# A three-stage graph kernel on one core: the last four tiles of the last quarter in 384 and 128 columns instead of 256 and 256, and the closing work in groups of 4, 3 and 1 row blocks instead of 4, 2 and 2

## The chip, the core and the metric

One core of a Trainium2 chip runs the kernel. The metric is the time of one execution on the device in microseconds (us); the figure for a kernel is the median of its runs.

## What is computed

The input is a node table x of 4096 x 128 and an adjacency matrix of 4096 x 4096, both float32, with small weights. Cut to what matters:

```python
def conv(x, a, eps, W, b):
    ax = a @ x
    h = ax + (1.0 + eps[0]) * ax
    for i in range(3):
        h = relu(h @ W[i].T + b[i])
    return h
merged = concatenate((conv(x, adj, ...), conv(x2, adj, ...)), axis=1)
x = layernorm(x + merged @ Wm.T + bm)
A_hat = adj + eye(4096)
d = where(deg > 0, rsqrt(deg), 0)          # deg: row sums of A_hat
x = layernorm(x + (d[:, None] * A_hat * d[None, :]) @ x @ W.T + b)
```

The second layer is the one that matters here: a product of the whole matrix with a 4096 x 128 table, a 128 x 128 projection, a residual and a layer norm over each row.

## The kernel before

**Tiling.** The 4096 output rows are cut into four quarters of 1024 rows (QUARTERS, QW). The products are made transposed: the stationary operand is a 128 x 128 block of the table, the moving operand is a stretch of the matrix, 128 contraction rows by up to 512 output rows (CW), and a PSUM bank `ps[...]` collects 128 features by 512 output rows. The words "columns" below are columns of the moving operand, so output rows of the result. A matrix tile in SBUF is 128 x 1024. To keep float32 accuracy, every operand is split into a rounded high part and the rest: ScalarE (ACT) rounds a tile into `ahi` or `hhi` (L626), VectorE (DVE) subtracts to get `alo` or `alo_extra` (L791), and TensorE (PE) makes three products, high by high, low by high and high by low, all in the type float32r, each with its own weight load.

**Order of the work.** Each engine has one instruction stream, written out by hand, and semaphores join them. First come four quarters of layer 0 (aggregation, three dense layers, merge), then four of layer 1. While a quarter of a layer streams its 32 tiles, the closing work of the quarter before is interleaved at fixed tile numbers. The matrix tiles arrive through SyncE's queue (SP) into a ring.

**The last quarter.** Here nothing follows that could hide the closing work, so the order is another one (`last_quarter` in the tensor stream). The 1024 output rows are two chunks of 512. Tiles 0 to 15 hold all 32 contraction blocks for the first chunk, two blocks per tile, tiles 16 to 31 the same for the second chunk, so `unit_products` (L524) issues 2 x 3 = 6 matmuls per tile. The first chunk is closed at tile 16 and projected (`project`, L510) while the second one streams. The last four tiles (SPLIT = 4) are walked through twice. The first walk ("half 0") takes their first TW columns and finishes output rows 0 to TW-1 of the chunk in `ps3`. The second walk ("half 1") takes the other columns, in a fresh bank `ps0`; since `ps3` already holds those columns of the tiles before, ACT copies both parts out (L758 for the first TW columns, L759 for the rest) and DVE adds `ps0` to the second part at the end (L1055, once per block of 128).

**The closing work** runs on row blocks of 128, eight in a quarter. TAIL names three groups: group 0 is the first chunk (blocks 0 to 3), group 1 the blocks that half 0 finishes, group 2 those that half 1 finishes. PE projects group 1 between the first and the second tile of half 1, and group 2 one block at a time after the add of L1055. DVE then does, for each group: `z` (L1061) per block, the statistics (L1066, L872) per block, and the variance plus epsilon (`vareps`, L879). GpSimd (POOL) raises it to the power -0.5 (`rstd`, L1090). For groups 0 and 1 DVE makes a shift (`nshift`, L884), ACT writes the normalised blocks into `outn` (L764) and SP stores them (L410). For group 2 DVE does the last step itself (L1075). The order in the DVE stream is fixed: group 1 up to its `vareps`, the shift of group 0, the add of L1055, the shift of group 1, then group 2:

```python
            for g, (k0, k1) in enumerate(TAIL):
                if g == 2:
                    ...
                    for k in range(k0, k1):
                        at = (k - HB) * P
                        dve.tensor_tensor(h[:, 1, at:at + P], ps[0][:, at - TW:at - TW + P], h[:, 1, at:at + P],
                                          ALU.add).then_inc(ay_added, 1)
                    shifts(2 * QUARTERS + 1, slice(*TAIL[1]))
```

Of the kernel before, what the change touches and what calls it, by code (L numbers as in the profile page):

```python
# [27 lines left out]
P = 128  # L28
# [7 lines left out]
CW = 512  # L36
# [9 lines left out]

QUADS = tuple((0, 1, LAST * 2 + c) + tuple(m for m in range(2, JB // 4) if m != LAST * 2 + c) for c in range(CH))
HALF_UNITS = JB // CH
TW = CW // 2

TAIL = ((0, 4), (4, 6), (6, 8))
TINY = 1.1754944e-38


# [58 lines left out]
def build(nc, a_t, head, early, x12, params, out):  # L113
    with ExitStack() as ctx:  # L114
# [3 lines left out]
        def sem(name):  # L118
            return ctx.enter_context(nc.semaphore(name))
# [50 lines left out]
        ps = [ctx.enter_context(nc.psum_tensor(f"ps{i}", [P, CW], F32)) for i in range(M)]  # L170
        pd = ctx.enter_context(nc.psum_tensor("pd", [P, M, CW], F32))
        merged = pd[:, 0:2, :].rearrange("p c (k d) -> p (c k) d", d=P)

        merged_last = lambda k: pd[:, 1 + max(k + 1 - TAIL[2][0], 0), (k % 4) * P:(k % 4 + 1) * P] if k >= HB else merged[:, k, :]
        totals = pd[:, 2, 0:QW // TB]
# [51 lines left out]
        out_written = sem("out_written")  # L227
        tail_ready = [sem(f"tail_ready{g}") for g in range(len(TAIL))]
        tail_written = sem("tail_written")
# [42 lines left out]
        def unit(n):  # L272

            c, i = n // HALF_UNITS, n % HALF_UNITS
            return c, 4 * QUADS[c][i // 2] + 2 * (i % 2)
# [23 lines left out]
        def ring_hi(layer, q, n):  # L299

            i = slot(layer, q, n)
            if i >= SPLIT:
                m = 2 * (i - SPLIT)
                return hhi[:, m:m + 2, :].rearrange("p m w -> p (m w)")
            return ahi[:, i, :]

        def ring_lo(layer, q, n):

            i = slot(layer, q, n)
            return alo_extra[:, i - SPLIT, :] if i >= SPLIT else alo[:, i, :]  # L310
# [24 lines left out]
        def _(sp):  # L335
# [63 lines left out]
            for m in range(PAIRS):  # L399
# [5 lines left out]
                for r, done in enumerate((unit_in[s], landed)):  # L405
                    sp.dma_start(dst[:, r, :].rearrange("p (t w) -> p t w", w=CW),
                                 a_t[pair + r][:, :, c * CW:(c + 1) * CW]).then_inc(done, 16)
            for g, (k0, k1) in enumerate(TAIL):
                sp.wait_ge(tail_ready[g], 1)
                sp.dma_start(out[LAST][:, k0 * P:k1 * P], outn[:, k0 * P:k1 * P]).then_inc(tail_written, 16)  # L410
            sp.wait_ge(tail_written, 16 * len(TAIL))


        @block.tensor
        def _(pe):
# [88 lines left out]
            def project(q, chunks=CH, blocks=range(KB)):  # L504

                wait(pe, ay_copied, q * CH + chunks)
                pe.wait_ge(z_ready, q + QUARTERS)
                for k in blocks:
                    to, first = (merged_last(k), blocks[0]) if q is LAST else (merged[:, k, :], k - k % 4)
                    mm = pe.matmul(to, h[:, k // 4, (k % 4) * P:(k % 4 + 1) * P],  # L510
                                   par[:, WO_AT:WO_AT + P], start=(k == first),
                                   stop=(k % 4 == 3 or k == blocks[-1]), skip_group_check=True)
                mm.then_inc(project_done, 1)

            def unit_products(n, cols, open_bank, bank, opens, closes):

                c, j = unit(n)
                hi, lo = ring_hi(1, LAST, n), ring_lo(1, LAST, n)
                for t in range(2):
                    at = slice(t * CW + cols.start, t * CW + cols.stop)  # L520
                    for k, (w, a) in enumerate(((x1hi, hi), (x1lo, hi), (x1hi, lo))):
                        if open_bank and t == 0 and k == 2:
                            pe.wait_ge(lo_ready, (QUARTERS + LAST) * JB + n + 1)
                        mm = pe.matmul(bank, block_of(w, j + t), a[:, at], start=(n == opens and t == 0 and k == 0),  # L524
                                       stop=(n == closes and t == 1 and k == 2), skip_group_check=True)
                return mm

            def last_quarter():

                for n in range(JB - SPLIT):  # L530
                    c = n // HALF_UNITS
                    pe.wait_ge(hi_ready, (QUARTERS + LAST) * JB + n + 1)
                    if n % HALF_UNITS == 0:
                        pe.wait_ge(ay_copied, (LAST - 2) * CH + c + 1)
                    mm = unit_products(n, slice(0, CW), True, ps[CH + c][:, :], c * HALF_UNITS, (c + 1) * HALF_UNITS - 1)
                    mm.then_inc(block_used, 1)
                    if n == PE_PROJECT:
                        project(LAST - 1)
                    if n == HALF_UNITS + PE_PROJECT + 1:
                        project(LAST, 1, range(KB // CH))  # L540
                for half in range(2):
                    for n in range(JB - SPLIT, JB):
                        if half == 0:
                            pe.wait_ge(hi_ready, (QUARTERS + LAST) * JB + n + 1)
                        mm = unit_products(n, slice(half * TW, (half + 1) * TW), half == 0, ps[(3, 0)[half]][:, 0:TW],
                                           (None, JB - SPLIT)[half], JB - 1)
                        if half:
                            mm.then_inc(block_used, 1)
                            if n == JB - SPLIT:
                                project(LAST, 2, range(*TAIL[1]))  # L550
                    if half == 0:
                        mm.then_inc(ay_done, 1)
# [27 lines left out]
            for q in range(1, QUARTERS - 1):  # L580
                layer1_quarter(q, q - 1)
            last_quarter()
            for i, k in enumerate(range(*TAIL[2])):
                pe.wait_ge(ay_added, i + 1)
# [4 lines left out]
        def _(act):  # L589
# [167 lines left out]
            act.wait_ge(ay_done, LAST + 1)  # L757
            act.activation(h[:, 1, 0:TW], ps[3][:, 0:TW], ACT.Copy).then_inc(ay_copied, 1)  # L758
            act.activation(h[:, 1, TW:CW], ps[3][:, TW:CW], ACT.Copy).then_inc(ay_copied, 1)  # L759
            act.wait_ge(out_written, 16 * LAST)  # L760
# [9 lines left out]
        def _(dve):  # L770
# [278 lines left out]
            for g, (k0, k1) in enumerate(TAIL):  # L1049
                if g == 2:  # L1050
                    dve.wait_ge(ay_copied, LAST * CH + 3)
                    dve.wait_ge(block_used, 2 * QUARTERS * JB)
# [4 lines that stand above are left out]
# [103 lines left out]
```

## Time and profile before

| | us |
|---|---|
| median of three runs | 594.59 (594.35 to 595.46) |
| the profiled execution | 595.34 |
| its span in the trace | 593.5 |
| PE busy | 586.1 (99%) |
| DVE busy | 540.0 (91%) |
| ACT busy | 372.8 (63%) |
| POOL busy | 28.7 (5%) |

The profiled execution is 1.84 us longer than its span, which is what lies around the traced instructions. Times of day in the rows are microseconds from the start of the span. A matmul's row in a timeline has its start and the time from there to its modelled end; since matmuls overlap, the distance between two starts says what one costs in a stream. A row with a count (x4) merges instructions, and its time runs from the first start to the last end.

### The profile page before, as it was taken

What the parts mean: (1) busy time and instruction counts of PE and PEld (TensorE: products, weight loads), DVE (VectorE), ACT (ScalarE), POOL (GpSimd) and SP (SyncE); (2) the same over time, 40 slices, a digit from 0 to 9 for tenths busy, and PEclk for the clock granted to TensorE, in tenths of its full rate; (3) what the DMA queues carried; (4) which work ended last, traced back from release to release, by engine and by line L of the source; (5) the groups of instructions that cost most, each with busy time, mean ns of one, the idle gap of its engine ahead of it and who ended that gap; (6) DMA issues with size and microseconds to landing.
All of it is one profiled execution on the core that took longest, in us unless ns stands there. A gap on an engine that the chain in (4) does not pass through costs nothing.

```text
span 593.5 us, 7715 instructions
## 1 busy us (share of the span) xinstructions
PE 586.1 (99%) x2676; PEld 484.6 (82%) x2676; DVE 540.0 (91%) x677; ACT 372.8 (63%) x494; POOL 28.7 (5%) x31
## 2 busy tenths in 40 slices
PE   8999999999999999999999999999999999999996
PEld 7788888888888888888888888867888888888885
DVE  5999999997987998898799999995899999989986
ACT  6643537752454773363667336476897888898893
POOL 1000000001100000110000020000200010010011
PEclk9999999999999999999999999999999999999998
DMA  8967665444555543454534475775699999999911
GB/s 331 391 246 284 213 214 212 142 142 142 197 180 194 175 172 145 141 188 173 204 141 141 142 273 185 286 306 224 238 358 407 354 362 390 401 362 375 388 48 71
DMA packets 27833, 141.56 MB, mean 239 GB/s; under 512 B 2592, under 2 KB 3360, under 8 KB 13600
## 3 DMA queue, kind: packets, MB, share of 16 engines
q1 hardware_dynamic: 27104, 139.41, 63.2%
q10 hardware_dynamic: 704, 1.84, 0.8%
q8 instruction: 14, 0.23, 0.2%
q14 instruction: 11, 0.09, 0.0%
HBM read 139.14 MB, written 2.10 MB: 238 GB/s over the span
## 4 chain that ended last, share of the span: by engine, by line
PE 94%; DVE 4%; DMA 1%; issue 0%; ACT 0%; SPq 0%; POOLq 0%; POOL 0%; DVEq 0%
PE ps L448 77%; PE ps L524 7%; PE pd L466 6%; PE pd L477 2%; DVE alo L791 1%; PE pd L510 1%; DMA raw<-early 1%; DVE rowsum L802 1%; DVE rowsum L806 1%; DVE x2s L775 0%; DVE x1lo L775 0%; DVE rowsum L799 0%; ACT ahi L626 0%; SPq L347 0%; POOLq L114 0%
## 5 line engine op out<-in xcount | busy, mean ns | idle before, releaser
L626 ACT ACTIVATE ahi<-raw 128x1024 fp32r<-128x1024 f32 x213 | 223.1, 1057 | 170.1 <-PE ps L448 156.0
L791 DVE TENSOR_TENSOR alo<-raw,ahi 128x1024 fp32r<-128x1024 f32 x213 | 257.9, 1218 | 31.6 <-ACT ahi L626 29.8
L448 PE MATMUL ps<-ahi,x2s 128*128 128x512 f32 x512 | 138.2, 389 | 0.0
L448 PE MATMUL ps<-ahi,x1hi 128*128 128x512 f32 x384 | 122.1, 394 | 0.5 <-ACT ahi L605 0.3
L448 PE MATMUL ps<-ahi,x1lo 128*128 128x512 f32 x384 | 120.5, 390 | 0.0
L448 PE MATMUL ps<-alo,x1hi 128*128 128x512 f32 x384 | 120.3, 389 | 0.0
L448 PEld LDWEIGHTS ps<-ahi,x2s 128*128 128x128 f32 x512 | 96.1, 188 | 20.1
L448 PEld LDWEIGHTS ps<-ahi,x1hi 128*128 128x128 f32 x384 | 71.8, 188 | 17.2 <-DVE x2s L775 1.4
L448 PEld LDWEIGHTS ps<-alo,x1hi 128*128 128x128 f32 x384 | 72.2, 188 | 15.2 <-DVE alo L783 0.2
L448 PEld LDWEIGHTS ps<-ahi,x1lo 128*128 128x128 f32 x384 | 72.2, 188 | 15.0
L448 PE MATMUL ps<-alo,x2s 128*128 128x512 f32 x256 | 80.1, 389 | 0.0
L802 DVE TENSOR_TENSOR rowsum<-rowsum,raw 128x1024 f32<-128x1024 f32 x60 | 72.9, 1215 | 0.0
L806 DVE TENSOR_TENSOR rowsum<-rowsum,raw 128x1024 f32<-128x1024 f32 x56 | 68.0, 1215 | 0.0
L791 DVE TENSOR_TENSOR alo_extra<-raw,hhi 128x1024 fp32r<-128x1024 f32 x42 | 50.6, 1219 | 6.8 <-ACT hhi L626 6.4
L448 PEld LDWEIGHTS ps<-alo,x2s 128*128 128x128 f32 x256 | 48.0, 188 | 10.0
L626 ACT ACTIVATE hhi<-raw 128x1024 fp32r<-128x1024 f32 x42 | 43.6, 1052 | 9.4 <-PE ps L448 8.2
L1090 POOL TENSOR_TENSOR rstd<-vareps,halves 128x8 f32<-128x8 f32 (+2 forms) x10 | 19.4, 1937 | 251.4 <-DVE vareps L985 145.1
L647 ACT ACTIVATE h<-pd,par 128x512 f32<-128x512 f32 x48 | 31.1, 680 | 0.4 <-PE pd L466 0.3
L811 DVE TENSOR_TENSOR hlo<-h,hhi 128x512 fp32r<-128x512 f32 x36 | 22.6, 681 | 0.0
L631 ACT ACTIVATE hhi<-h 128x512 fp32r<-128x512 f32 x36 | 22.1, 629 | 0.8
L1085 POOL TENSOR_TENSOR degpow<-degc,halves 128x8 f32<-128x8 f32 x4 | 6.7, 1670 | 309.0 <-DVE degpos L850 309.0
L448 PE MATMUL ps<-hhi,x1hi 128*128 128x512 f32 x64 | 20.6, 398 | 0.0
(97 smaller groups left out, 507.9 us busy)
## 6 DMA issues: line engine op xcount, KB each, us to landing
raw<-a_t SPq DMA_DIRECT2D x108, 1024.0 KB, 4.9
raw<-a_t SPq DMA_DIRECT2D x32, 512.0 KB, 7.3
raw<-early SPq DMA_DIRECT2D x7, 512.0 KB, 8.3
xn<-x SPq DMA_DIRECT2D x3, 1024.0 KB, 8.6
out<-outn ACTq DMA_DIRECT2D x3, 512.0 KB, 6.8
par<-params SPq DMA_DIRECT2D x1, 708.0 KB, 13.5
raw<-head SPq DMA_DIRECT2D x2, 256.0 KB, 3.3
xn<-x SPq DMA_DIRECT2D x1, 512.0 KB, 8.3
```

Of the source, the lines that this page charges most:

```text
L448: mm = pe.matmul(ps[bank + (CH * (q % 2) if layer else 0)][:, :], block_of(w, n), a[c], start=(n == 0 and k == 0), stop=(n == JB - 1 and k ...
L466: mm = pe.matmul(pd[:, m, :], w[:, at:at + P], a[:, m, :], start=(k == 0), stop=(k == len(passes) - 1))
L477: mm = pe.matmul(merged[:, k, :], h[:, CH * b + k // 4, (k % 4) * P:(k % 4 + 1) * P], par[:, WM_AT + b * P:WM_AT + (b + 1) * P], start=(k ...
L524: mm = pe.matmul(bank, block_of(w, j + t), a[:, at], start=(n == opens and t == 0 and k == 0), stop=(n == closes and t == 1 and k == 2), s ...
L626: act.activation(ring_hi(layer, q, n), raw_tile(layer, n), ACT.Copy).then_inc(hi_ready, 1)
L631: act.activation(hhi[:, m, :], h[:, m, :], ACT.Copy).then_inc(hhi_ready, 1)
L647: act.activation(h[:, m, :], pd[:, m, :], ACT.Relu, bias=par[:, at:at + 1]).then_inc(h_ready, 1)
L791: dve.tensor_tensor(ring_lo(layer, q, n), raw_tile(layer, n), as_f32(ring_hi(layer, q, n)), ALU.subtract).then_inc(lo_ready, 1)
L802: dve.tensor_tensor(rowsum[:, :], rowsum[:, :], tile, ALU.add).then_inc(rowsum_step, 1)
L806: dve.tensor_tensor(to[:, :], rowsum[:, :], tile, ALU.add).then_inc(raw_used, 1)
L811: dve.tensor_tensor(hlo[:, m, :], h[:, m, :], as_f32(hhi[:, m, :]), ALU.subtract).then_inc(hlo_ready, 1)
L1090: pool.tensor_tensor(rstd[:, r], vareps[:, r], halves[:, r], ALU.pow).then_inc(rstd_ready, 1)
```

## The change

TW becomes 384, so half 0 takes 384 columns of the last four tiles and half 1 takes 128. TAIL becomes (0, 4), (4, 7), (7, 8), so group 1 has three row blocks and group 2 has one. The tensor stream's slices follow these two sizes.

```diff
-TW = CW // 2
-
-TAIL = ((0, 4), (4, 6), (6, 8))
+TW = CW - P
+
+TAIL = ((0, 4), (4, 7), (7, 8))
@@ last_quarter
-                        mm = unit_products(n, slice(half * TW, (half + 1) * TW), half == 0, ps[(3, 0)[half]][:, 0:TW],
+                        mm = unit_products(n, slice(*((0, TW), (TW, CW))[half]), half == 0, ps[(3, 0)[half]][:, 0:(TW, CW - TW)[half]],
                                            (None, JB - SPLIT)[half], JB - 1)
```

On PE, around the projection of group 1 in half 1 (`pd<-par,h` is the projection), before:

```order
L524 MATMUL ps<-alo_extra,x1hi 128x256
L510 MATMUL pd<-par,h 128x128 x2
L524 MATMUL ps<-hhi,x1hi 128x256
L524 MATMUL ps<-hhi,x1lo 128x256
L524 MATMUL ps<-alo_extra,x1hi 128x256
```

and now:

```order
L524 MATMUL ps<-alo_extra,x1hi 128x128
L510 MATMUL pd<-par,h 128x128 x3
L524 MATMUL ps<-hhi,x1hi 128x128
L524 MATMUL ps<-hhi,x1lo 128x128
L524 MATMUL ps<-alo_extra,x1hi 128x128
```

The 24 matmuls of half 1 have half the columns, and one projection has moved from the very end into the middle of the walk. The 24 of half 0 read 128x384 in place of 128x256.

On DVE, from group 1 to the end of the program, before:

```order
L1061 SCALAR_TENSOR_TENSOR z<-pd,dall,xn 128x128 x2
L1066 BN_STATS stats<-z 128x6 x2
L872 BN_AGGR mv<-stats 128x2 x2
L879 TENSOR_SCALAR vareps<-mv 128x2
L884 SCALAR_TENSOR_TENSOR nshift<-mv,rstd 128x4
L1055 TENSOR_TENSOR h<-ps,h 128x128 x2
L884 SCALAR_TENSOR_TENSOR nshift<-mv,rstd 128x2
L1061 SCALAR_TENSOR_TENSOR z<-pd,dall,xn 128x128 x2
L1066 BN_STATS stats<-z 128x6 x2
L872 BN_AGGR mv<-stats 128x2 x2
L879 TENSOR_SCALAR vareps<-mv 128x2
L1075 TENSOR_SCALAR outn<-z,mv,rstd 128x128 x2
```

and now:

```order
L1061 SCALAR_TENSOR_TENSOR z<-pd,dall,xn 128x128 x3
L1066 BN_STATS stats<-z 128x6 x3
L872 BN_AGGR mv<-stats 128x2 x3
L879 TENSOR_SCALAR vareps<-mv 128x3
L884 SCALAR_TENSOR_TENSOR nshift<-mv,rstd 128x4
L1055 TENSOR_TENSOR h<-ps,h 128x128
L884 SCALAR_TENSOR_TENSOR nshift<-mv,rstd 128x3
L1061 SCALAR_TENSOR_TENSOR z<-pd,dall,xn 128x128
L1066 BN_STATS stats<-z 128x6
L872 BN_AGGR mv<-stats 128x2
L879 TENSOR_SCALAR vareps<-mv 128x1
L1075 TENSOR_SCALAR outn<-z,mv,rstd 128x128
```

One block's instructions have moved from behind the add of L1055 to ahead of it. On ACT seven blocks are normalised in place of six, and the two copies are 384 and 128 wide. The stores of groups 1 and 2 have 192 KB and 64 KB in place of 128 KB each.

## Rows read from the trace of the kernel before

**Rows 1.** Chain of waits, two pieces: start us, us, what.

```profile
540.41 2.72 PE ps L524 x12
...
587.69 2.35 issue
```

**Rows 2.** Timeline of PE, last four tiles: start us, us, engine line op out<-in.

```profile
581.04 0.28 PE L524 MATMUL ps<-hhi,x1hi 128*128 128x256 f32 x1
...
583.91 0.28 PE L524 MATMUL ps<-hhi,x1hi 128*128 128x256 f32 x1
...
584.63 0.63 PE L510 MATMUL pd<-par,h 128*128 128x128 f32 x4
...
585.22 0.28 PE L524 MATMUL ps<-hhi,x1lo 128*128 128x256 f32 x1
...
587.12 0.28 PE L524 MATMUL ps<-alo,x1hi 128*128 128x256 f32 x1
```

**Rows 3.** Timeline of PE and its weight loads, merge of layer 0, quarter 0.

```profile
132.66 1.08 PEld L477 LDWEIGHTS pd<-par,h 128*128 128x128 f32 x9
...
132.55 0.19 PE L474 MATMUL pd<-partial,same_place 128*128 128x32 f32 x1
...
132.57 0.28 PE L474 MATMUL pd<-partial,same_place 128*128 128x32 f32 x1
```

**Rows 4.** Chain of waits, the merge of layer 0, quarter 0.

```profile
132.85 3.65 PE pd L477 x32
```

**Rows 5.** Timeline of ACT, copies out of PSUM and the last normalisation.

```profile
565.78 0.58 ACT L741 ACTIVATE h<-ps 128x512 f32<-128x512 f32 x1
...
584.11 0.38 ACT L758 ACTIVATE h<-ps 128x256 f32<-128x256 f32 x1 [2.86 <-PE ps L524]
...
587.07 2.42 ACT L764 ACTIVATE outn<-z,nshift,rstd 128x128 f32<-128x128 f32 x6 [2.30 <-DVE nshift L884]
```

**Rows 6.** Timeline of DVE, closing work; idle before and its releaser in brackets.

```profile
582.43 1.12 DVE L1061 SCALAR_TENSOR_TENSOR z<-pd,dall,xn 128x128 f32<-128x128 f32 x4
...
584.91 0.17 DVE L879 TENSOR_SCALAR vareps<-mv 128x4 f32<-128x4 f32 x1
585.30 0.61 DVE L1061 SCALAR_TENSOR_TENSOR z<-pd,dall,xn 128x128 f32<-128x128 f32 x2 [0.22 <-PE pd L510]
...
586.74 0.17 DVE L879 TENSOR_SCALAR vareps<-mv 128x2 f32<-128x2 f32 x1
586.82 0.15 DVE L884 SCALAR_TENSOR_TENSOR nshift<-mv,rstd 128x4 f32<-128x4 f32 x1
587.51 0.49 DVE L1055 TENSOR_TENSOR h<-ps,h 128x128 f32<-128x128 f32 x2 [0.54 <-PE ps L524]
587.92 0.15 DVE L884 SCALAR_TENSOR_TENSOR nshift<-mv,rstd 128x2 f32<-128x2 f32 x1
588.38 0.61 DVE L1061 SCALAR_TENSOR_TENSOR z<-pd,dall,xn 128x128 f32<-128x128 f32 x2 [0.32 <-PE pd L510]
...
589.83 0.17 DVE L879 TENSOR_SCALAR vareps<-mv 128x2 f32<-128x2 f32 x1
590.81 0.60 DVE L1075 TENSOR_SCALAR outn<-z,mv,rstd 128x128 f32<-128x128 f32 x2 [0.81 <-POOL rstd L1090]
```

**Rows 7.** Timeline of POOL, the powers of groups 0 and 1.

```profile
585.16 1.01 POOL L1090 TENSOR_TENSOR rstd<-vareps,halves 128x4 f32<-128x4 f32 x1 [12.13 <-DVE vareps L879]
586.99 0.70 POOL L1090 TENSOR_TENSOR rstd<-vareps,halves 128x2 f32<-128x2 f32 x1 [0.83 <-DVE vareps L879]
```

**Rows 8.** SP's last issue in the timeline; stores with KB each and us to landing.

```profile
591.44 0.33 SPq L410 DMA_DIRECT2D out<-outn  x1
...
out<-outn SPq DMA_DIRECT2D x1, 256.0 KB, 2.1
out<-outn SPq DMA_DIRECT2D x2, 128.0 KB, 1.7
```

**Rows 9.** Busy time in a stretch: us, engines busy (count), granted clock, DMA, GB/s.

```profile
588.00:588.60 0.60, 0.57 (x4) 0.38 (x4) 0.28 (x2) 0.60 (x2) 0.00 (x0) 1.00 0.00 0
```

## The prediction

> **What bounds the kernel now.** The page's shares come first: PE is busy for 99% of the span, so only two things can move the time, the columns that PE streams and the closing work that starts when PE has stopped. The change leaves every matmul of the program in place up to the last four tiles, so I read only the last 13 us. The chain of waits is the next view. It walks PE until the projection of group 1 and then shows a piece of 2.35 us called issue, in which nothing is released [rows 1]. That piece is the warning: the chain took a side path (group 1's power on POOL), and the engines' timelines must say what really happened there. They do. The last matmul of half 1 starts at 587.12 [rows 2]; DVE, idle for 0.54 us, starts the add of L1055 at 587.51 with PE as its releaser, `z` of group 2 at 588.38 after the projection, `vareps` at 589.83 and the final normalisation at 590.81 [rows 6]; SP issues the last store at 591.44, and it needs 1.7 us to land [rows 8]. So today the end hangs on PE: add at 587.51, then 3.93 us to the issue. DVE had finished group 1 at 586.74 + 0.17 = 586.91 and the shift of group 0 by 586.97 [rows 6]: it was early by about half a microsecond. That slack is what the change spends.
>
> **PE, half 0.** A 512-column matmul costs 2.72 / 12 = 0.227 us in a stream [rows 1], one with 256 columns (583.91 - 581.04) / 24 = 0.120 us [rows 2]. The line through both gives 0.173 us for 384. Half 0 starts at 581.04 and ends its issue at 581.04 + 24 x 0.173 = 585.2.
>
> **PE, half 1.** No float32r matmul with 128 columns is in the trace, so its price is bounded. Below: the line through 512 and 256 gives 0.066 us. Above: a float32 matmul with 128 columns is two passes, 32 passes in 3.65 us [rows 4], so 0.114 each and 0.23 per matmul. Between them stands the weight load, one per matmul. In the merge nine loads take 1.08 us, and with the 0.19 us of one taken off, eight distances of 0.111 us [rows 3]. That it is the load and not the stream is seen at the two passes with only 32 columns: they end at 132.55 + 0.19 = 132.74 and 132.57 + 0.28 = 132.85, again 0.11 apart [rows 3]. I take 0.115, between this pace and today's 0.120: halving the columns frees next to nothing. The Trainium skill (TensorE: Matmul & The Clock Gate, "Back-to-back issue gap") gives about 81 ns for a sustained stream of load and matmul pairs at 128 columns; the load pace of this trace speaks against so low a value for 4-byte weights. By that figure PE would be done 0.6 us sooner than I say, and the time would be the same, for DVE is then the only bound; it makes the tie below safer.
>
> The projection of group 1 now waits for a 384-column copy. ACT starts it 0.20 us after half 0 (583.91 to 584.11 now) at 585.4; between 0.38 for 256 columns and 0.58 for 512 I take 0.48 [rows 5]; PE follows 0.14 after its end, at 586.0. The first tile of half 1 has been issued by 585.2 + 6 x 0.115 = 585.9, so PE stands still for 0.1. From there: four passes took 585.22 - 584.63 - 0.12 = 0.47 us [rows 2], six take 0.70; the other 18 matmuls take 18 x 0.115 = 2.07; PE has issued all at 588.8, against 587.24 now. The add follows 0.27 later (587.24 to 587.51), less 0.05 for the shorter last stream: **589.0 by PE**.
>
> **DVE, group 1.** From the start of the projection to `z` it takes 0.67 us (584.63 to 585.30), and two more passes 0.22: `z` at 586.9. From `z` to `vareps` two blocks need 586.74 - 585.30 = 1.44 and four 584.91 - 582.43 = 2.48 [rows 6], so 0.52 a block and 1.96 for three: `vareps` at 588.87, the shift of group 0 at 588.95, and the add can start at **589.03 by DVE**. Both engines come to the same instant, 1.5 us later than now. A quicker stream on PE would therefore gain nothing: the slack of half a microsecond is gone, and DVE is what is late next.
>
> **A new wait.** Behind the add DVE has the shift of group 1, which needs `rstd`. POOL starts 0.25 after `vareps` (586.74 to 586.99), takes 0.70 for two columns and 1.01 for four, so 0.85 for three [rows 7]: 588.87 + 0.25 + 0.85 = 589.97, and the shift starts at 590.0. Today it starts right behind the adds at 587.92 [rows 6] with `rstd` there since 587.69. Queued behind it in DVE's stream is `z` of group 2, which PE has ready at 589.03 + 0.87 = 589.9 but which now starts at 590.1, one step of 0.08 behind the shift. Now it is 588.38: **+1.7**.
>
> **What the last group saves.** One block less: 0.52 up to `vareps`, (1.01 - 0.70) / 2 = 0.16 on POOL, and (0.60 - 0.34) = 0.26 of the last normalisation, whose single instruction takes about 0.34 like each `z`; together 0.94 us. The second add is not in this sum: it ran beside the first projection. So the last block is ready at 591.41 + 1.7 - 0.94 = 592.2, against 591.41.
>
> **ACT and the stores.** ACT starts the normalisations 0.25 after the shift of group 0 (586.82 to 587.07 now), so at 589.2. Six take 2.42 us; with 0.48 for the last, 0.39 apart [rows 5]. Seven are done at 589.2 + 6 x 0.39 + 0.48 = 592.0, where now they are done at 589.49, far ahead of everything. So SP issues group 1's store at 592.05 and is occupied for 0.33 us [rows 8]; the last store, ready at 592.2, is issued at 592.4. 256 KB land in 2.1 us and 128 KB in 1.7 [rows 8]; by that slope 64 KB need 1.5 and 192 KB 1.9: both land near 593.9. Counted as one transfer of 256 KB from 592.05 it would be 594.15. Today the last one lands at 591.44 + 1.7 = 593.14. I take +0.85 us, with ends of +0.7 and +1.0 from these two counts. The Trainium skill (DMA: Bandwidth & Descriptors, the two cost components of an issued DMA) has about 2.0 us whatever the size, plus bytes / 436 GB/s. The rows disagree with its constant (1.7 us for 128 KB, all told) and agree that size matters little; with its slope the halved last store is 0.15 us shorter, not 0.2, which would put the sum 0.05 higher.
>
> Edits without a price: the clock stays granted in full while PE projects the last group (1.00 from 588.00 to 588.60 [rows 9]), and the gap before that projection is no longer than now. ACT's second copy (L759) is narrower and done long before the add. Group 0 is untouched until the shift.
>
> **The sum** stands against the profiled execution, 595.34 us with a span of 593.5: the span becomes about 594.35 and that execution 596.2. The median of the runs is 0.75 lower than the profiled one, so the median goes from 594.59 to 595.4. I call a difference under 0.2%, 1.19 us, no difference; that is about what a measurement of this kernel can tell. The forecast is +0.14%, on the slower side of no difference. With 0.120 per matmul instead of 0.115, and the ends of the store, this case reaches from 594.9 to 596.0.
>
> **Rivals.**
> A. Narrow matmuls are dear (the slower side). If float32r with 128 columns costs what float32 costs, 0.228 us, half 1 decides: first tile done at 586.6, projections 0.70, 18 x 0.228 = 4.1, add at 591.6, `z` at 592.5, the issue 2.1 later at 594.6 against 591.44, stores no longer on each other's heels and the last one 0.2 shorter: +3.0, so 597.6. It decides as soon as the add comes later than 590.1 - 0.87 = 589.2, which is at 0.125 us per matmul. For it: nothing in the trace shows float32r narrower than 256 columns, and the nearest form of 128 columns, float32, does cost that. Against: up to there its price falls in line with the columns, and the load pace gives no reason for a rise.
> B. ACT does not keep its pace of 0.39 between normalisations, or two stores at once cost more than one of 256 KB. At 0.48 each, seven end at 592.56, the stores are issued at 592.6 and 592.95 and land at 594.5: +1.4, 596.0. For it: ACT and DVE then work at the same time on `z` and `outn`. Against: they do so now, and the pace is 0.39.
> C. The saving comes through. With 0.066 per matmul PE's add would come at 588.2; if DVE were also there by then, the sum is +0.7 - 0.94 and a little for the store: 594.3, and 593.4 if the add did not move at all. Against: DVE would have to do 1.96 us of group 1 in 1.2, and each step of it is in the rows.
> D. The change does not act (the groups reach the end as before): 594.6. The order of instructions speaks against it.
>
> **Chances.** Forecast 0.62, A 0.18, B 0.13, C 0.05, D 0.02. The range of 594.3 to 596.8 leaves out A and the far end of C, 0.2. Faster by over 0.2% needs C in full: 0.03. No difference: 0.54 of the forecast's 0.62, 0.03 of B, 0.02 of C, D, together 0.61. Slower: 0.08 of the forecast (its high end passes 595.78), A, 0.10 of B: 0.36.
>
> **What would show it.** In the profile after: starts in half 0 0.173 apart; in half 1 0.11 to 0.12; `z` of group 1 near 586.9 with three blocks; the add near 589.0 with next to no idle time before it; the shift of group 1 idle before it, released by POOL; `z` of group 2 at 590.1; SP's last two issues back to back near 592.2. The prediction is wrong if half 1's matmuls stand 0.2 apart, if the add comes before 588.5, or if the shift of group 1 doesn't wait.

## The result and the profile after

| | before | after |
|---|---|---|
| median, 20 runs each, us | 595.06 (594.35 to 595.76) | 596.15 (595.71 to 597.31) |
| ratio | | 1.002, 95% interval 1.0013 to 1.0026 |
| span of the profiled execution, us | 593.5 | 594.0 |
| first matmul of half 0, from the start | 581.04 | 580.43 |
| from there to the span's end, from unrounded times | 12.51 | 13.55 |

The change costs 1.1 us, 0.2%. The forecast was +0.8 (0.14%) from a median of 594.59, to 595.4; the measured 596.15 lies in the range given, 0.75 above the point.

The last two lines of the table carry the comparison. The two programs do the same work up to the first matmul of half 0, yet it stands 0.61 us earlier in the trace of the changed kernel. The chain of waits of each kernel shows a difference of the same size at the start of the program, in the first load: 5.38 us in the changed kernel and 5.99 in the kernel before.

```profile
1.67 5.38 DMA raw<-early
```

```profile
1.67 5.99 DMA raw<-early
```

(The first line is from the kernel after, the second from the kernel before.) So two spans may differ by half a microsecond for a reason that has nothing to do with the change. From here on I count from the first matmul of half 0 and call the distance to the span's end the **tail**: 12.51 before, 13.55 after, +1.04. The views print a span to 0.1 us only, and from such spans the two would be 12.46 and 13.57, the figures that the expectations below go by; the tails in this text are taken from the trace's own unrounded times.

The timeline of PE after (start us, us, engine line op), the first matmuls of half 0, of half 1, and the last one:

```profile
580.43 0.33 PE L524 MATMUL ps<-hhi,x1hi 128*128 128x384 f32 x1
...
584.61 0.22 PE L524 MATMUL ps<-hhi,x1hi 128*128 128x128 f32 x1
584.67 0.27 PE L524 MATMUL ps<-hhi,x1lo 128*128 128x128 f32 x1
584.78 0.27 PE L524 MATMUL ps<-alo_extra,x1hi 128*128 128x128 f32 x1
584.89 0.28 PE L524 MATMUL ps<-hhi,x1hi 128*128 128x128 f32 x1
585.00 0.28 PE L524 MATMUL ps<-hhi,x1lo 128*128 128x128 f32 x1
585.12 0.27 PE L524 MATMUL ps<-alo_extra,x1hi 128*128 128x128 f32 x1
585.35 0.94 PE L510 MATMUL pd<-par,h 128*128 128x128 f32 x6
...
587.98 0.27 PE L524 MATMUL ps<-alo,x1hi 128*128 128x128 f32 x1
```

Half 0 takes (584.61 - 580.43) / 24 = 0.174 us a matmul, half 1 0.111, against 0.120 for either before [rows 2].

The first two matmuls of half 1 stand only 0.06 us apart, so 128 columns need no more than that. The timeline of the weight loads (PEld) shows what the later ones keep step with:

```profile
584.61 0.19 PEld L524 LDWEIGHTS ps<-hhi,x1lo 128*128 128x128 f32 x1
584.72 0.19 PEld L524 LDWEIGHTS ps<-alo_extra,x1hi 128*128 128x128 f32 x1
584.83 0.19 PEld L524 LDWEIGHTS ps<-hhi,x1hi 128*128 128x128 f32 x1
```

The loads begin 0.11 us apart, and each matmul begins 0.06 behind its own load (584.61 and 584.67, 584.72 and 584.78).

The timeline of DVE after, to be held against [rows 6]; the brackets say how long DVE was idle and who ended it:

```profile
586.33 0.87 DVE L1061 SCALAR_TENSOR_TENSOR z<-pd,dall,xn 128x128 f32<-128x128 f32 x3 [1.86 <-PE pd L510]
587.23 0.68 DVE L1066 BATCH_NORM_STATS2 stats<-z 128x6 f32<-128x128 f32 x3
587.94 0.31 DVE L872 BATCH_NORM_AGGREGATE mv<-stats 128x2 f32<-128x6 f32 x3
588.29 0.17 DVE L879 TENSOR_SCALAR vareps<-mv 128x3 f32<-128x3 f32 x1
588.37 0.15 DVE L884 SCALAR_TENSOR_TENSOR nshift<-mv,rstd 128x4 f32<-128x4 f32 x1
588.44 0.28 DVE L1055 TENSOR_TENSOR h<-ps,h 128x128 f32<-128x128 f32 x1
589.42 0.16 DVE L884 SCALAR_TENSOR_TENSOR nshift<-mv,rstd 128x3 f32<-128x3 f32 x1 [0.70 <-POOL rstd L1090]
589.50 0.35 DVE L1061 SCALAR_TENSOR_TENSOR z<-pd,dall,xn 128x128 f32<-128x128 f32 x1
590.43 0.15 DVE L879 TENSOR_SCALAR vareps<-mv 128x1 f32<-128x1 f32 x1
591.25 0.35 DVE L1075 TENSOR_SCALAR outn<-z,mv,rstd 128x128 f32<-128x128 f32 x1 [0.66 <-POOL rstd L1090]
```

The add of L1055 has lost its bracket: DVE goes into it without idle time, where PE ended 0.54 us of it before. The shift of group 1 has gained one, released by POOL. The idle time was moved, not removed.

ACT, and SP's last two issues in their timelines; then the stores with the time to landing:

```profile
588.62 2.80 ACT L764 ACTIVATE outn<-z,nshift,rstd 128x128 f32<-128x128 f32 x7 [3.15 <-DVE nshift L884]
```

```profile
591.45 0.35 SPq L410 DMA_DIRECT2D out<-outn  x1
591.84 0.43 SPq L410 DMA_DIRECT2D out<-outn  x1
```

```profile
out<-outn SPq DMA_DIRECT2D x1, 192.0 KB, 1.9
out<-outn SPq DMA_DIRECT2D x1, 64.0 KB, 1.7
```

The last block is ready at 591.25 + 0.35 = 591.60, the last issue comes 0.24 us later, behind the one for group 1. The last store lands 1.04 us later than before, counted from half 0; 1.01 of it is the later issue (11.41 against 10.40).

### The profile page after: what moved, and what is told of

It reads as the page before. It is cut to its first block, busy times and chain, and to the rows that moved or that the text cites. A ratio compares the mean times of both kernels' runs of the same rounds, so it can differ in the third digit from the quotient of the medians.

```text
span 594.0 us, 7713 instructions
## 1 busy us (share of the span) xinstructions
PE 586.7 (99%) x2676; PEld 485.4 (82%) x2676; DVE 539.6 (91%) x675; ACT 372.9 (63%) x495; POOL 28.7 (5%) x31
## 4 chain that ended last, share of the span: by engine, by line
PE 94%; DVE 4%; DMA 1%; issue 0%; ACT 0%; POOL 0%; SPq 0%; POOLq 0%
PE ps L448 77%; PE ps L524 7%; PE pd L466 6%; PE pd L477 2%; DVE alo L791 1%; PE pd L510 1%; DMA raw<-early 1%; DVE rowsum L802 1%; DVE rowsum L806 1%; DVE x2s L775 0%; DVE x1lo L775 0%; DVE rowsum L799 0%; ACT ahi L626 0%; DVE z L1061 0%; POOL rstd L1090 0%
## 5 line engine op out<-in xcount | busy, mean ns | idle before, releaser
L1090 POOL TENSOR_TENSOR rstd<-vareps,halves 128x8 f32<-128x8 f32 (+3 forms) x10 | 19.4, 1938 | 252.4 <-DVE vareps L985 145.1
```

The source lines that it names most:

```text
L1090: pool.tensor_tensor(rstd[:, r], vareps[:, r], halves[:, r], ALU.pow).then_inc(rstd_ready, 1)
```

## The experiments

The differences looked for are tenths of a microsecond, and the start of the program moves by more than that, so beside each ratio to the kernel before I give the tail of the profiled execution. Such tails repeat closely: the kernel before and before_more, whose last issue is at the same place, both have 12.51, and the kernel after, after_cut and narrow64 have 13.55, 13.55 and 13.56. Each run below the first two has 7 to 11 executions (narrow64 one), and its ratio is to executions of the kernel before made beside it, whose medians were 594.97 to 595.09. before_cut, after_cut and narrow64 leave out a part of the products, so their output is not that of the full work.

| kernel | median us, ratio to before (95%) | add at | z of last group | last issue | tail |
|---|---|---|---|---|---|
| before | 595.06 | 6.47 | 7.34 | 10.40 | 12.51 |
| after | 596.15, 1.002 (1.0013 to 1.0026) | 8.01 | 9.07 | 11.41 | 13.55 |
| before_cut | 594.48, 0.9993 (0.9983 to 1.0002) | 5.86 | 6.76 | 9.81 | 11.92 |
| after_cut | 596.03, 1.0017 (1.0008 to 1.0027) | 8.01 | 9.07 | 11.41 | 13.55 |
| before_more | 595.04, 0.9997 (0.9987 to 1.0007) | 6.47 | 7.34 | 10.40 | 12.51 |
| after_more | 596.19, 1.0024 (1.0012 to 1.0035) | 8.59 | 9.66 | 12.00 | 14.14 |
| late_shift | 596.43, 1.0019 (1.001 to 1.0028) | 8.01 | 8.88 | 11.41 | 13.56 |
| act_store | 596.17, 1.0017 (1.0008 to 1.0026) | 8.01 | 9.07 | 11.18 | 13.56 |
| both_moves | 596.06, 1.0013 (1.0004 to 1.0023) | 8.02 | 8.88 | 11.00 | 13.51 |
| cols_alone | 596.15, 1.0019 (1.001 to 1.0028) | 7.93 | 8.81 | 11.60 | 13.71 |
| narrow64 | 596.20, one execution | 8.01 | 9.08 | 11.41 | 13.56 |
| early_shift | 595.78, 1.0015 (1.0005 to 1.0024) | 7.95 | 9.08 | 11.19 | 13.18 |
| early_late | 595.76, 1.001 (1.0001 to 1.0019) | 7.94 | 8.82 | 10.96 | 13.09 |
| pool_norm | 595.27, 1.0002 (0.9993 to 1.0011) | 6.47 | 7.34 | 10.74 | 12.85 |

### Who holds the add: less work on PE, more on DVE

The first pair leaves out 8 of half 1's 24 matmuls, those with the low part of the table, in the kernel before and in the changed one (`skip` is a new argument of `unit_products`, empty elsewhere).

```diff
                     for k, (w, a) in enumerate(((x1hi, hi), (x1lo, hi), (x1hi, lo))):
+                        if k in skip:
+                            continue
...
-                                           (None, JB - SPLIT)[half], JB - 1)
+                                           (None, JB - SPLIT)[half], JB - 1, (1,) if half else ())
```

> The kernel before, half 1 without its products of the low part of the table (8 of its 24 matmuls of 256 columns are left out, so the last rows lose a part of their accuracy). Times are counted from the first matmul of half 0; in the kernel before, the add of L1055 starts at 6.47, z of the last group at 7.34, the last store is issued at 10.40 and the span ends at 12.46. If PE sets the end there and DVE is early by half a microsecond, the add moves until DVE's order stops it: to 6.0, z to 6.87, the issue to 9.93, and the time falls by 0.5 us against before. If something behind PE sets the end, nothing moves.

> The changed kernel with the same 8 matmuls of half 1 left out (128 columns each). In the changed kernel the add starts at 8.01, the shift of group 1 at 8.99, z of the last group at 9.07, the last issue is at 11.41 and the span ends at 13.57. Main theory: DVE's work on three blocks and POOL's power hold the end, PE is only level with them; PE ends some 0.8 us sooner and nothing else moves, 0.0 us against the changed kernel. Rival: the narrow matmuls are what costs the time; then the add comes up to 0.8 us sooner and the time falls by 0.5 or more.

The timeline of DVE, before_cut:

```profile
586.90 0.16 DVE L886 SCALAR_TENSOR_TENSOR nshift<-mv,rstd 128x4 f32<-128x4 f32 x1
586.98 0.48 DVE L1057 TENSOR_TENSOR h<-ps,h 128x128 f32<-128x128 f32 x2
587.80 0.16 DVE L886 SCALAR_TENSOR_TENSOR nshift<-mv,rstd 128x2 f32<-128x2 f32 x1 [0.35 <-POOL rstd L1092]
```

In the kernel before, the add moved from 6.47 to 5.86 and stopped where DVE's order stopped it, right behind the shift of group 0; and at once the wait for POOL appeared that the change also has. The tail fell by 0.59, the median by 0.49 (594.97 beside it). In the changed kernel the last matmul of half 1 came at 6.88 instead of 7.55, and no other time moved: add 8.01, tail 13.55. PE does not hold the end there.

The second pair makes group 1's statistics twice.

```diff
+                if g == 1:
+                    for k in range(k0, k1):
+                        dve.bn_stats(partial[:, 6 * (k - k0):6 * (k - k0) + 6], z[:, k, :])
                 for k in range(k0, k1):
                     dve.bn_stats(stats[:, k, :], z[:, k, :]).then_inc(stats_step, 1)
```

> The kernel before with group 1's statistics made twice on DVE (the first time into a tile that nothing reads): 2 x 0.19 = 0.38 us more ahead of the add. Main theory: DVE has half a microsecond of slack there, so the add stays at 6.47 and the time is that of before, +0.0. Rival (DVE's work in the tail adds up whatever PE does): +0.38 us.

> The changed kernel with group 1's statistics made twice: 3 x 0.19 = 0.57 us more on DVE ahead of the add. Main theory: no slack is left, the add, the shift of group 1 and everything behind come 0.57 us later: add at 8.6, z of the last group at 9.65, last issue at 12.0, and the time is 0.55 us above the changed kernel. Rival (PE sets the end): +0.1 or less, since PE and DVE would have to differ by half a microsecond.

The same extra work is free in one kernel (add at 6.47, last issue at 10.4, both as before) and costs its full length in the other (add, z and last issue 0.58 or 0.59 later, tail +0.59). The medians do not show it: the expected 0.55 us is missing there, after_more's median is 0.04 above the changed kernel's and 0.16 above that of after_cut, which ran beside it. Its seven executions lie between 595.73 and 597.16, and the profiled one, the fastest, reached half 0 at 579.80, 0.63 us before the changed kernel's. So the two theories are told apart by the trace alone.

### What the waits behind the add cost

```diff
-                    shifts(2 * QUARTERS + 1, slice(*TAIL[1]))
...
                 i.then_inc(z_ready, 1)
+                if g == 2:
+                    shifts(2 * QUARTERS + 1, slice(*TAIL[1]))
```

> The changed kernel with one instruction moved on DVE: the shift of group 1 stands behind z of the last group instead of ahead of it, so z no longer waits for POOL. z of the last group comes at 8.88 instead of 9.07 from the first matmul of half 0, and the last block is ready 0.19 us sooner. Theory of the stores (SP is still busy with group 1's store until 11.37): the last issue stays near 11.4 and the time is the same, 0.0. Theory of the chain on DVE: the last issue moves to 11.2 and the time falls by 0.19 us.

The timeline of DVE, late_shift:

```profile
589.74 0.35 DVE L1060 SCALAR_TENSOR_TENSOR z<-pd,dall,xn 128x128 f32<-128x128 f32 x1 [0.58 <-PE pd L510]
590.00 0.15 DVE L884 SCALAR_TENSOR_TENSOR nshift<-mv,rstd 128x3 f32<-128x3 f32 x1
```

z is now released by PE and comes at 8.88, as worked out, and the last block is ready 0.20 sooner. The tail is 13.56, the same. The gain ended at SP:

```profile
591.88 0.82 SPq L410 DMA_DIRECT2D out<-outn  x2
```

The two issues stand in one piece of 0.82 us, so the last one waits for the one before it (591.88 is 11.02 from half 0, where ACT has finished its seventh block).

```diff
             for g, (k0, k1) in enumerate(TAIL):
+                if g == 1:
+                    continue
                 sp.wait_ge(tail_ready[g], 1)
...
+            act.wait_ge(tail_ready[1], 1)
+            k0, k1 = TAIL[1]
+            act.dma_start(out[LAST][:, k0 * P:k1 * P], outn[:, k0 * P:k1 * P]).then_inc(tail_written, 16)
```

> The changed kernel with the store of group 1 issued by ACT behind its last normalisation, in place of SP. SP is then free when the last block is ready: its issue comes at 11.21 instead of 11.41. Theory of the stores: -0.2 us. If instead the landing of group 1's 192 KB ends the span, 0.0.

> Both of these edits in the changed kernel: the last issue at 11.02, 0.39 us sooner than in the changed kernel. Group 1's store is then issued at about the same time and needs 1.9 us for 192 KB, 12.9, against 12.7 for the last one: it ends the span, at 13.4 in place of 13.57, so -0.2 us, not -0.39. A chain on DVE alone would give -0.39.

The last issue moved as expected (11.18, and 11.00 with both edits), but the tail did not: 13.56 and 13.51, against 13.55. act_store met its second alternative, 0.0, though not for the reason given with it, and both_moves missed its -0.2. The issues and the stores' landings say where the gain went. act_store:

```profile
591.89 0.34 ACTq L771 DMA_DIRECT2D out<-outn  x1
```

```profile
592.05 0.35 SPq L412 DMA_DIRECT2D out<-outn  x1
```

```profile
out<-outn ACTq DMA_DIRECT2D x1, 192.0 KB, 1.9
out<-outn SPq DMA_DIRECT2D x1, 64.0 KB, 2.0
```

both_moves:

```profile
out<-outn ACTq DMA_DIRECT2D x1, 192.0 KB, 2.1
out<-outn SPq DMA_DIRECT2D x1, 64.0 KB, 1.7
```

Sent at nearly the same moment on two queues, one of the two stores takes 0.2 to 0.3 us longer than in the changed kernel: 64 KB 2.0 instead of 1.7, or 192 KB 2.1 instead of 1.9. Count instead from the first of the two issues to the last landing. From unrounded times that is 2.12 us in the changed kernel, 2.12 in act_store, and 2.10 in both_moves, where the 192 KB store lands last. One store of 256 KB takes 2.0 to 2.1. So these two stores land as one of 256 KB would, from the moment the first of them is issued, on one queue or on two. What inside the transfers makes them wait for each other no run shows. The end then hangs on the time of the first issue, 11.02, whoever issues it, and that is late because ACT begins its seven normalisations only after the shift of group 0. This led to the next edit.

```diff
-                if g == 1:
+                if g == 0:
                     shifts(2 * QUARTERS, slice(*TAIL[0]))
```

> The changed kernel with the shift of group 0 ahead of group 1's work on DVE, which idles there for 1.86 us. ACT then normalises group 0 from 5.4 on (from the first matmul of half 0), group 1 from 9.2, and is done at 10.5 instead of 11.0; the add is ready on both engines at 7.94. SP is free when the last block is ready: last issue at 11.21 instead of 11.41, and group 1's store has landed by 12.5 and no longer disturbs it. Theory of the late stores: span end at 13.35, -0.2 us against the changed kernel. If the last store's landing alone counts as in the run with ACT's issue: no change.

> The same with the shift of group 1 behind z of the last group as well. z of the last group at 8.82, last block ready at 10.93, last issue at 11.0, landing 1.7 later: span end at 13.16, -0.4 us against the changed kernel. That removes every wait that the change added behind the add, and what stays against the kernel before is PE's later add less the block saved: +0.7 us. So even then it is not faster than before.

The timelines of DVE and ACT, early_late:

```profile
585.91 0.16 DVE L884 SCALAR_TENSOR_TENSOR nshift<-mv,rstd 128x4 f32<-128x4 f32 x1 [1.12 <-POOL rstd L1091]
586.65 0.87 DVE L1060 SCALAR_TENSOR_TENSOR z<-pd,dall,xn 128x128 f32<-128x128 f32 x3 [0.57 <-PE pd L510]
```

```profile
586.17 1.65 ACT L764 ACTIVATE outn<-z,nshift,rstd 128x128 f32<-128x128 f32 x4 [0.38 <-DVE nshift L884]
590.02 1.26 ACT L764 ACTIVATE outn<-z,nshift,rstd 128x128 f32<-128x128 f32 x3 [2.20 <-DVE nshift L884]
```

The shift of group 0 fits into idle time of DVE, ACT does four of its seven blocks 2.8 us sooner, and the tail falls to 13.18, with the late shift of group 1 as well to 13.09, where 13.35 and 13.16 were expected. The first two lines are early_shift's stores, the other two early_late's:

```profile
out<-outn SPq DMA_DIRECT2D x1, 192.0 KB, 1.9
out<-outn SPq DMA_DIRECT2D x1, 64.0 KB, 1.6
```

```profile
out<-outn SPq DMA_DIRECT2D x1, 192.0 KB, 1.9
out<-outn SPq DMA_DIRECT2D x1, 64.0 KB, 1.7
```

In early_shift group 1's store goes out at 10.48, 0.71 us ahead of the last one, and 64 KB land in 1.6. In early_late it goes out at 10.56, only 0.39 ahead, and the pair needs 2.12 us again. Of the 1.04 us that the change adds to the tail, 0.46 was in this order of DVE's stream and of the stores behind it. The other 0.58 stays when no wait for POOL stands between the add and z of the last group, and it fits two numbers: the add 7.94 - 6.47 = 1.47 later, the block saved 0.94.

### Columns alone, and what a narrow matmul costs

```diff
-TAIL = ((0, 4), (4, 7), (7, 8))
+TAIL = ((0, 4), (4, 6), (6, 8))
...
-                    for k in range(k0, k1):
+                    for k in range(HB + TW // P, k1):
                         at = (k - HB) * P
...
                                 project(LAST, 2, range(*TAIL[1]))
+                                project(LAST, 2, (TAIL[2][0],))
...
-            for i, k in enumerate(range(*TAIL[2])):
+            for i, k in enumerate(range(HB + TW // P, KB)):
```

> The columns alone: half 0 with 384, half 1 with 128, but the groups stay 4, 2 and 2. Block 6 is projected in the middle of half 1 behind the two of group 1, and needs no add; its z and its statistics stay in the last group. Group 1's z comes at 5.7 from the first matmul of half 0, its vareps at 7.1, so DVE is early and PE's add sets the pace, at 7.9; z of block 7 at 8.8, and from there the last group costs what it cost before less the first z: last issue at 11.6, +1.2 against the kernel before, +0.2 against the changed one in issue, and with 128 KB to land about +0.2 in time. If the groups were the cause of the loss, this would be near the kernel before.

The timeline of DVE, cols_alone:

```profile
588.35 0.29 DVE L1056 TENSOR_TENSOR h<-ps,h 128x128 f32<-128x128 f32 x1 [0.57 <-PE ps L524]
```

With two blocks in group 1 DVE is idle for 0.57 us ahead of the add, and PE releases it at 7.93. That is PE's own time with the new columns, which the changed kernel hides behind DVE's 8.01. The two were 0.08 apart. Of the 1.46 us by which PE's add is late, 1.31 are the wider half 0 (it ends 4.18 after its start, against 2.87); half 1, with narrower matmuls and one projection more, takes the other 0.15. The tail is 13.71, 0.15 above the changed kernel: the groups of three and one blocks are not the cause of the loss, they win back a little of what the columns cost.

The next run changes two pieces of one line, shown without the rest of it:

```diff
-slice(*((0, TW), (TW, CW))[half])
+slice(*((0, TW), (TW, TW + 64))[half])
-[:, 0:(TW, CW - TW)[half]]
+[:, 0:(TW, 64)[half]]
```

> The changed kernel with the matmuls of half 1 cut to 64 columns (the other 64 rows of the last block lose the last four tiles). In the changed kernel those of 128 columns start 0.111 us apart. If the weight load sets that pace, 64 columns also start 0.111 apart. Rival: a narrow float32r matmul pays twice per column (2 x 128 / 2.4 GHz is 0.107 too); then 64 columns start about 0.06 apart.

The timeline of PE, narrow64, in half 1:

```profile
586.99 0.28 PE L524 MATMUL ps<-alo_extra,x1hi 128*128 128x64 f32 x1
587.10 0.28 PE L524 MATMUL ps<-ahi,x1hi 128*128 128x64 f32 x1
587.22 0.28 PE L524 MATMUL ps<-ahi,x1lo 128*128 128x64 f32 x1
587.33 0.28 PE L524 MATMUL ps<-alo,x1hi 128*128 128x64 f32 x1
```

64 columns start 0.11 us apart, like 128. So in this stream of one weight load per matmul the width no longer matters at 128 columns and below, and the pace is that of the loads, which begin 0.11 us apart in both kernels.

### A try at the kernel before

```diff
-            for k in range(*TAIL[2]):
+            for k in range(TAIL[2][0] + 1, TAIL[2][1]):
...
+            pool.wait_ge(rstd_ready, 2 * QUARTERS + 2)
+            pool.wait_ge(out_written, 16 * LAST)
+            k = TAIL[2][0]
+            pool.tensor_scalar(outn[:, k * P:(k + 1) * P], z[:, k, :], mv[:, k, 0:1], rstd[:, k:k + 1],
+                               ALU.subtract, ALU.mult).then_inc(tail_ready[2], 1)
...
-                sp.wait_ge(tail_ready[g], 1)
+                sp.wait_ge(tail_ready[g], 2 if g == 2 else 1)
```

> Not the change but a try at the kernel before: of the last group's two final normalisations one is given to POOL, which has just made the power, so that DVE does one instead of two. DVE then ends 0.26 us sooner. If POOL needs about 0.3 us for a 128x128 block, as its other passes over 128x128 do, the last issue comes 0.2 us sooner and the span ends at 12.25 instead of 12.46. If POOL is slower than 0.6 us or both slow each other down, nothing is gained or it is slower.

The timeline of POOL:

```profile
591.09 0.87 POOL L1122 TENSOR_SCALAR outn<-z,mv,rstd 128x128 f32<-128x128 f32 x1
```

POOL needs 0.87 us for the block, DVE 0.60 for both. The last issue came 0.34 later, and so did the tail (12.85). My figure of 0.3 was taken from another operation, and it did not carry over. No run that does the whole work beats the kernel before.

## Why the prediction was right, point by point

**The number.** The point was 595.4, the median came out at 596.15. 0.47 us of that gap is the starting point: the median of three executions of the kernel before was 594.59, that of twenty 595.06. The rest is the change itself, +0.81 said and +1.09 measured. The range of 594.3 to 596.8 is more than twice as wide as the effect, and one rival's figure, B's 596.0, is nearer than the forecast's; so the steps below, not the median, show that the mechanism was right.

**PE, half 0 and half 1.** 0.173 was 0.174. 0.115, taken between a load pace of 0.111 and 0.120, was 0.111, and the loads' own timeline and the narrow64 run bear out the reason given for it. Rival A, with its 0.23, is out, and C's 0.066 too. The figure of 81 ns in the Trainium skill (TensorE: Matmul & The Clock Gate, "Back-to-back issue gap") is not met by this stream: 111 ns.

**The tie.** Said: 589.0 by PE and 589.03 by DVE, counted from half 0 at 581.04, so 7.96 and 7.99. Measured: 7.93 by PE (cols_alone) and 8.01 by DVE. The two pairs of runs show that the half microsecond of slack on DVE is gone: the same cut on PE gives 0.59 before and nothing after, the same kind of extra work on DVE costs nothing before and 0.59 after.

**The new wait.** Said: shift of group 1 at 8.96, z at 9.06. Measured: 8.99 with POOL as releaser, and 9.07. Removed alone, in late_shift, it gives nothing back, since the stores hold the end.

**What the last group saves.** From z to the last block ready it took 10.37 - 7.34 = 3.03 before and 11.17 - 9.07 = 2.10 now, 0.93 less; said 0.94.

**ACT and the stores.** Said: seven blocks done at 10.96, last issue at 11.36. Measured: 588.62 + 2.80 gives 10.99, and 11.41. Neither half of rival B occurred: ACT kept its pace of 0.38 to 0.39, and the two stores took 2.1 us together, as one of 256 KB does.

**The term that was mis-sized** is the landing of the last store. The prediction had two counts. By the slope between 256 and 128 KB, 64 KB need 1.5 us and the end moves by 0.76; as one transfer of 256 KB from the first issue it moves by 1.0. I took +0.85, nearer the lower. The upper one is what happened, +1.04: the last store landed 2.1 us after group 1's was issued, so its own 64 KB took 1.7. That is not what 64 KB cost: 0.71 us behind the other store they took 1.6 (early_shift). The choice between the two counts was not argued, and act_store and both_moves now decide it. The Trainium skill (DMA: Bandwidth & Descriptors, the two cost components) has the larger part of such a transfer independent of its size, a fit that the page gives for DMAs issued by GpSimd. The stores here, issued by SP, agree with its slope: from 64 to 256 KB they go from 1.6 to 2.0 or 2.1, and the page's slope gives 0.45 us for these 192 KB, an estimate. They do not have its constant of 2.0 us, since 64 KB land in 1.6 all told.

**The bound between no difference and slower.** The measured ratio, 1.002, stands on it, with an interval of 1.0013 to 1.0026, so the measurement does not decide between the two. The forecast had 0.14%, and gave the slower side 0.36.

## What to carry to other kernels

When a closing stage is cut smaller so that less hangs behind the last matmul, put the work that has moved forward against the slack of the engine it moves to, and look at what that engine's stream has queued behind it: here 0.94 us saved at the end was paid with 1.5 us ahead of it. Narrowing a matmul that loads its own weights saves next to nothing once the load sets the pace (0.111 us at 128 and at 64 columns, 0.120 at 256), while the columns that it gives up are paid in full elsewhere. Look also at two stores that leave close together at the end: here they landed as one of their joint size, so only an earlier start of the first one helped. And where the start of a program varies by more than the difference looked for, measure each trace from a common instruction close to the change.

## What the runs showed that was not expected

Two stores issued within 0.2 us of each other on two queues, 192 KB and 64 KB, did not land sooner than one behind the other on one queue: the last issue moved forward by 0.41 us (11.41 to 11.00) and the tail by 0.05. The pair took 2.1 us from the first issue to the last landing in four kernels (after, act_store, both_moves, early_late). A store of 64 KB took 1.6, 1.7 or 2.0 us, by whether the one of 192 KB was issued 0.71, 0.39 or 0.16 us before it. POOL's normalisation of a 128x128 block took 0.87 us, against 0.35 on DVE.
